# Head 0's later probability tile: normalised and turned by VectorE instead of GpSimd and TensorE

## The reference

```python
scores = jnp.einsum('bnhd,bmhd->bhnm', q, k) * scale
mask = jnp.tril(jnp.ones((n, n), bool))
scores = jnp.where(mask[None, None], scores, -jnp.inf)
p = jax.nn.softmax(scores, axis=-1)
o = jnp.einsum('bhnm,bmhd->bnhd', p, v).reshape(b, n, H * D)
```

## Time and profile before

| | |
|---|---|
| median of three runs | 1040.01 us |
| profiled execution, its own time | 1039.91 us |
| its span, first to last instruction | 1038.1 us |
| granted TensorE clock | 0.997 |
| first L1580 to the last of 128 | 27.1 to 825.7 us |
| eight steps, from L1580 to L1580 | 50.0 to 50.8 us |

### The profile page before, as it was taken

One profiled execution on the slowest core, in us unless ns is written; L12 is line 12 of the kernel. 1 busy time (PEld: TensorE's weight loads), 2 busy tenths in 40 slices (PEclk: granted clock), 3 DMA queues, 4 the chain that ended last, 5 costly groups with the idle time before them and its releaser, 6 DMA issues.

```text
span 1038.1 us, 25078 instructions
## 1 busy us (share of the span) xinstructions
PE 1021.4 (98%) x7827; PEld 981.6 (95%) x7827; DVE 827.1 (80%) x2841; ACT 868.2 (84%) x2399; POOL 931.4 (90%) x926
## 2 busy tenths in 40 slices
PE   7999999999999999999999999999999999999996
PEld 6899999999999999999999999999999999999996
DVE  6868888878887888788888888887777767677776
ACT  5988898989898989898989898889898867877774
POOL 4899999999999999999999999999999847877775
PEclk9999999999999999999999999999999999999998
DMA  7561121112112110121122112111131000000001
GB/s 262 187 184 43 42 63 41 43 52 68 44 36 61 63 42 33 62 63 42 33 68 67 42 39 75 43 42 53 42 113 31 2 1 11 22 24 29 22 22 41
DMA packets 35124, 58.56 MB, mean 56 GB/s; under 512 B 3136, under 2 KB 16000, under 8 KB 34688
## 3 DMA queue, kind: packets, MB, share of 16 engines
q1 hardware_dynamic: 34992, 56.96, 17.2%
HBM read 50.92 MB, written 9.18 MB: 58 GB/s over the span
## 4 chain that ended last, share of the span: by engine, by line
POOL 60%; PE 19%; issue 14%; DVE 1%; POOLq 0%; ACT 0%; ACTq 0%; DVEq 0%
POOL arena L599 15%; POOL arena L622 14%; POOL arena L633 13%; POOL arena L609 13%; PE psum L1017 12%; PE psum L1057 6%; POOL arena L581 1%; POOL arena L557 1%; POOL X L590 1%; PE psum L775 1%; PE psum L1030 1%; POOL arena L565 0%; PE psum L1039 0%; POOLq L303 0%; POOL arena L572 0%
## 5 line engine op out<-in xcount | busy, mean ns | idle before, releaser
L633 POOL TENSOR_TENSOR arena<-arena 128x768 f32<-128x768 f32 x128 | 196.2, 1533 | 8.9 <-DVE arena L1580 8.3
L609 POOL TENSOR_TENSOR arena<-arena 128x512 f32<-128x512 f32 x128 | 174.0, 1359 | 10.0
L1593 DVE SCALAR_TENSOR_TENSOR pt_split<-psum,vh_col,pt_split 128x256 fp32r<-128x256 f32 (+1 forms) x512 | 177.0, 407 | 3.5 <-ACT pt_split L1252 3.0
L599 POOL TENSOR_TENSOR arena<-arena,tables 128x512 f32<-128x512 f32 x128 | 166.9, 1304 | 13.7 <-ACT arena L1222 13.0
L622 POOL TENSOR_TENSOR arena<-arena 128x512 f32<-128x512 f32 x127 | 162.9, 1283 | 0.0
L929 PE MATMUL psum<-arena 128*128 128x256 f32 x512 | 153.9, 382 | 3.1 <-POOL arena L609 1.8
L775 PE MATMUL psum<-wo_hi,o_hi 128*128 128x256 f32 x512 | 152.1, 297 | 0.0
L1233 ACT ACTIVATE arena<-arena 128x256 f32<-128x256 f32 x256 | 128.6, 502 | 26.7 <-DVE arena L1570 20.1
L775 PE MATMUL psum<-xt_lo,wq_hi 128*128 128x256 f32 x512 | 144.7, 283 | 0.0
L775 PE MATMUL psum<-xt_hi,wq_lo 128*128 128x256 f32 x512 | 144.5, 282 | 0.0
L775 PE MATMUL psum<-wo_hi,o_lo 128*128 128x256 f32 x512 | 144.3, 282 | 0.0
(11 more groups left out here) (195 smaller groups left out, 3405.7 us busy)
## 6 DMA issues: line engine op xcount, KB each, us to landing
arena<-kh_rows SPq DMA_DIRECT2D x127, 256.0 KB, 3.3
out<-spare SPq DMA_DIRECT2D x15, 256.0 KB, 2.1
arena<-w_rows SPq DMA_DIRECT2D x6, 512.0 KB, 4.8
X<-L_attn_Wout SPq DMA_DIRECT2D x1, 2048.0 KB, 14.5
X<-L_attn_x SPq DMA_DIRECT2D x1, 2048.0 KB, 12.5
arena<-L_attn_Wq SPq DMA_DIRECT2D x1, 1536.0 KB, 10.0
X<-L_attn_x SPq DMA_DIRECT2D x1, 1536.0 KB, 9.7
w_rows<-L_ffn_w_gate_up SPq DMA_DIRECT2D x3, 512.0 KB, 8.2
```

What stands on the lines that cost most here:

```text
L599: nc.gpsimd.tensor_tensor(swap, swap, spread, ALU.mult).then_inc(q_sined, 1)
L609: nc.gpsimd.tensor_tensor(q_rot[p % 2], q_cos[p % 2], q_swap[p % 2], ALU.add).then_inc(q_roped, 1)
L633: nc.gpsimd.tensor_tensor(tb, tb, r.unsqueeze(3).to_broadcast([P, HP, 3, P]), ALU.mult).then_inc(p_ready, 1)
L1593: last = nc.vector.scalar_tensor_tensor(pt_lo[p % 2][:, o], b[:, i], vh[:, t, h:h + 1], pt_hi[p % 2][:, o].bitcast(F32), ALU.mult, ALU.sub ...
```

## The change

The later tile of the pair's first head (j = 0) leaves its old path. What is done now:

- The scores of head 0's later queries are written in another column order: the keys go through the PE in blocks of 32 columns ("b m c" order), and DVE's `maxima` uses a mask `mask_blocks` in that order.
- After the reciprocal, DVE multiplies this tile (128 x 256, in place in SBUF) by the reciprocal: `scale_late`, one TENSOR_SCALAR that waits for `p_inv`. It raises `p_scaled`.
- POOL's `normalise` covers the other 4 x 128 columns only and still waits for `p_inv`.
- SP issues four DMAs for each pair (`exchange`), SBUF to SBUF, 128 pieces of 256 bytes each, from `T` into the new tensor `blocks`, once `p_scaled` is there. They raise `p_exchanged`.
- In the next step, ahead of the next reciprocal, DVE turns `blocks` in 32 x 32 blocks into head 0's PSUM bank: `fill_pt`, one 128 x 256 transpose that waits for `p_exchanged` and for PE's one remaining transpose of head 0. It raises `pt_filled`.
- PE leaves out two of the six transposes of a pair; ACT's `split_pt` waits for `pt_filled` for head 0.

```diff
+            def exchange(g0, s):
+                at = pair_at(g0, s, LAG["softmax"])
+                if at:
+                    g, p, _ = at
+                    sp.wait_ge(p_scaled, g + 1)
+                    at_least(sp, pt_filled, g)
+                    for b in range(4):
+                        sp.dma_start(blocks[b * 32:(b + 1) * 32, :].rearrange("q (a e) -> q a e", a=4),
+                                     T[p % 2][:, 0, b * 64:(b + 1) * 64]).then_inc(p_exchanged, 16)
...
-                    tb = T[p % 2].rearrange("p j (c m) -> p j c m", m=P)
-                    r = rinv[p % 4].rearrange("p (j c) -> p j c", j=HP)[:, :, 0:3]
+                    tb = T[p % 2].rearrange("p j c -> p (j c)")[:, N:6 * P].rearrange("p (k m) -> p k m", m=P)
                     pool.wait_ge(p_inv, g + 1)
-                    nc.gpsimd.tensor_tensor(tb, tb, r.unsqueeze(3).to_broadcast([P, HP, 3, P]), ALU.mult).then_inc(p_ready, 1)
+                    nc.gpsimd.tensor_tensor(tb, tb, rinv[p % 4][:, 3:7].unsqueeze(2).to_broadcast([P, 4, P]), ALU.mult)\
+                        .then_inc(p_ready, 1)
...
-                        nc.tensor.matmul(sj[:, 0:2 * P], q[:, j, P:N], kt[:, j, :], start=True, stop=True,
+                        all_keys = kt[:, j, :] if j else kt[:, j, :].rearrange("p (m b c) -> p b m c", m=NT, b=4)
+                        nc.tensor.matmul(sj[:, 0:2 * P], q[:, j, P:N], all_keys, start=True, stop=True,
...
-                        nc.tensor.transpose(b[:, 0:P], tb[:, j, 2 * P:3 * P], ident[:, :])
-                        nc.tensor.transpose(b[:, P:2 * P], tb[:, j, 0:P], ident[:, :])
-                        nc.tensor.transpose(b[:, 2 * P:3 * P], tb[:, j, P:2 * P], ident[:, :]).then_inc(pt_ready, 1)
+                        last = nc.tensor.transpose(b[:, 0:P], tb[:, j, 2 * P:3 * P], ident[:, :])
+                        if j:
+                            nc.tensor.transpose(b[:, P:2 * P], tb[:, j, 0:P], ident[:, :])
+                            last = nc.tensor.transpose(b[:, 2 * P:3 * P], tb[:, j, P:2 * P], ident[:, :])
+                        last.then_inc(pt_ready, 1)
...
-                        act.wait_ge(pt_ready, head_count(g, j))
+                        act.wait_ge(*((pt_ready, head_count(g, j)) if j else (pt_filled, g + 1)))
...
                         at_least(dve, pt_ready, (g - 2) * HP + HP)
+                        at_least(dve, p_exchanged, (g - 2) * 64 + 64)
...
-                    nc.vector.tensor_tensor_reduce(tb[:, j, 0:2 * P], S_BANK[j][:, 0:2 * P], mask[:, :], -1.0, -MASKED,
+                    nc.vector.tensor_tensor_reduce(tb[:, j, 0:2 * P], S_BANK[j][:, 0:2 * P], (mask if j else mask_blocks)[:, :],
...
+            def scale_late(g0, s):
+                at = pair_at(g0, s, LAG["softmax"])
+                if at:
+                    g, p, _ = at
+                    late = T[p % 2][:, 0, 0:2 * P]
+                    dve.wait_ge(p_inv, g + 1)
+                    nc.vector.tensor_scalar(late, late, rinv[p % 4][:, 0:1], None, ALU.mult).then_inc(p_scaled, 1)
+
+            def fill_pt(g0, s):
+                at = pair_at(g0, s, LAG["turn"])
+                if at:
+                    g, p, _ = at
+                    dve.wait_ge(p_exchanged, g * 64 + 64)
+                    dve.wait_ge(pt_ready, head_count(g, 0))
+                    nc.vector.transpose(PT_BANK[0][:, P:3 * P].rearrange("p (m q a) -> p m a q", m=NT, a=4),
+                                        blocks[:, :].rearrange("p (a m c) -> p m a c", a=4, m=NT)).then_inc(pt_filled, 1)
...
+                    fill_pt(g0, s)
                     invert_sums(g0, s)
+                    scale_late(g0, s)
```

More of the change, by code:

```diff
@@ L109, in sandwich_kernel @@
         eps = sb("eps", [P, 1])
+        blocks = sb("blocks", [P, N])
+        mask_blocks = sb("mask_blocks", [P, N])
         cosq, sinq, cosk, sink = (tables[:, i, :] for i in range(4))
@@ L276, in sandwich_kernel @@
             sem(k) for k in ("s_ready", "s_max", "p_exp", "p_inv", "p_ready"))
+        p_scaled, p_exchanged, pt_filled = (sem(k) for k in ("p_scaled", "p_exchanged", "pt_filled"))
         pt_ready, pt_hi_done, pt_lo_done, o_ready, o_hi_done, o_lo_done, y_added = (
@@ L490, in batch @@
                         spread_kh(g0, s + KH_LEAD)
+                    exchange(g0, s)
                     if isinstance(g0, int) and g0 == 0 and s >= ROWS_STEP and s < ROWS_STEP + CHUNKS:
@@ L540, in _ @@
             nc.gpsimd.memset(minus_one, -1.0).then_inc(zeroed, 1)
-            pool.wait_ge(zeroed, 6)
+            nc.gpsimd.memset(mask_blocks[:, :], 0.0).then_inc(zeroed, 1)
+            pool.wait_ge(zeroed, 7)
             for m in (ident, ident_bf):
@@ L547, in _ @@
                                     pattern=[[-1, P]], channel_multiplier=1).then_inc(consts, 1)
+            late = mask_blocks[:, :].rearrange("p (b m c) -> p b m c", b=4, m=NT)[:, :, 1, :]
+            nc.gpsimd.affine_select(out=late, in_=late, compare_op=ALU.is_ge, fill=masked_fill, base=0,
+                                    pattern=[[-32, 4], [-1, 32]], channel_multiplier=1).then_inc(consts, 1)
             def invert_x(c0):
@@ L1134, in batch @@
                     early_unit_step(g0, s, step)
-            pe.wait_ge(consts, 3)
+            pe.wait_ge(consts, 2)
             keep_busy(F_BANK, 9)
@@ L1565, in maxima @@
                         at_least(dve, pt_ready, (g - 2) * HP + HP)
+                        at_least(dve, p_exchanged, (g - 2) * 64 + 64)
+                        if isinstance(g0, int) and g == 0:
+                            dve.wait_ge(consts, 4)
                     dve.wait_ge(s_ready, head_count(g, j))
                     nc.vector.memset(gate_mark[:, j:j + 1], 0.0)
-                    nc.vector.tensor_tensor_reduce(tb[:, j, 0:2 * P], S_BANK[j][:, 0:2 * P], mask[:, :], -1.0, -MASKED,
+                    nc.vector.tensor_tensor_reduce(tb[:, j, 0:2 * P], S_BANK[j][:, 0:2 * P], (mask if j else mask_blocks)[:, :],
+                                                   -1.0, -MASKED,
                                                    ALU.add, ALU.min, nmax[p % 4][:, 2 * j:2 * j + 1])
```

## The result

The changed kernel takes **1145.47 us** (median of 4 runs, 1145.14 to 1150.6), against 1040.07 us for the kernel before on the same chip. The ratio is 1.1023, with a 95% interval of 1.0999 to 1.1047: slower by 105.4 us. The forecast was 1155 us. The profiled execution has a span of 1143.6 us at a granted clock of 0.995, against 0.997 before, so TensorE's clock plays no part.

What follows compares the result with a forecast made beforehand. The prediction took a ring of waits between DVE and ACT, touched by PE at L1261, as the bound. 126 - 22 + 13 = 117 us on 1038.1, plus 1.8, gave 1157, stated as 1155; range 1040 to 1185.

Steps and rivals of the forecast that it cites:

- The exclusion: DVE's multiplication beside POOL's normalise: they exclude each other, so the multiplication ends 1.24 us after the reciprocal.
- One of the signs: In the profile after the change, PE would show gaps before L794; no size given.
- Who is first: At p_inv after the reciprocal: POOL starts after 0.08 us, DVE after 0.10, so POOL wins by 0.02; chance 0.45.
- DVE goes first: Rival at the reciprocal: DVE's multiplication starts before POOL's normalise, +55 us, 1095 us; chance 0.2.
- The sum: Whole kernel: 126 - 22 + 13 = 117 us added to a span of 1038.1 us.
- 159 - 33 - 22 = 104 us: DVE's multiplication: 128 x 1.24 = 159 us, less 33.2 idle before L1602, less 22 for 32 pairs with shorter waits.
- The turn: DVE's 32 x 32 transpose before the reciprocal: 0.42 us each, mostly in idle time, 13 us in all.
- PE's 28 us don't come off: PE's two dropped transposes per pair: 2 x 0.11 x 128 = 28 us of PE time, none of it gained.
- the ring: DVE and ACT waiting for each other set the pace, 5.63 us around in one step; PE touches it at L1261.
- The exchange is hidden: SP's four DMAs: exchanged at 4.5 us from the reciprocal's start, DVE needs it at 5.2; hidden by 0.6, costs nothing.
- No exclusion: Rival: DVE's multiplication runs at single rate through one port and doesn't exclude POOL; 1070 us, chance 0.17.
- Faster: Rival: PE is the bound and DVE's 211 us of idle time takes the new work; 1012 to 1020 us, chance 0.15.

Runs made afterwards that it cites:

- the experiment that makes it true: Changed kernel with DVE's multiplication also writing a row sum into a spare column, same operands, waits and place: 1065.21 us, ratio 1.0242.
- both-savings kernel: Kernel before with POOL's normalise on 512 columns and PE without two of six transposes, nothing in their place: 1018.11 us, ratio 0.9785.

## Why the prediction was right

**The exclusion was the main term, and its mechanism is shown** by four experiments: taking it away (two kernels) gives back 80.3 and 75.0 us, turning the order (two kernels) 74.3 and 77.1. The forecast had the multiplication end 1.24 us after the reciprocal. In the 95 pairs it ends 1.27 after it: normalisation from 0.079, 1.045 long, then 0.15. Uncontended it ends at 0.39 (forecast 0.35). One of the signs came out elsewhere: PE's gaps stand before its transposes (L966, 60.0 us), not before L794 (14.3 us).

The Trainium skill (SBUF — State Buffer, "Who interferes with whom") says that of the forms of tensor_scalar the one that also writes out its accumulator cannot enter the modes with both ports. The 479 ns beside POOL's 1043 agree with that rule, and the 1236 ns of the other form with its exclusive lock.

**Who is first: right by luck, from a wrong reading.** I let DVE's start come 0.10 us after the reciprocal, by the earlier trace rows, and POOL's 0.08, and gave POOL the port by 0.02 us. In the records L1616 starts 0.035 us after the reciprocal and POOL's L651 0.079, so DVE's record starts first by 0.044 us, and POOL still has the ports in 95 of 128 pairs. With POOL at 0.11 by its record, or at 0.16 by the memset's end, DVE has them. So the record's start doesn't say when DVE asks for the ports. If POOL's does, DVE asks later than 0.044 us after its own, and by 0.13 us at the latest; that is worked out from these three starts and not measured by itself. My margin of 0.02 us came out with the right sign, from a start (0.10 us) that L1616 doesn't show, and I had given this case no more than 0.45. *DVE goes first* was priced at 1095; the two kernels in which it is so measure 1071 and 1068. Of the 24 to 27 us too much, 12 are the remainders of L609, of which the mean of 508 ns leaves (508 - 353) x 128 = 20 us and not 32. The rest was not taken apart; slack that I didn't count, as in the sum below, is the likely part.

**The sum.** The multiplication stood in it with 159 - 33 - 22 = 104 us. Measured: mean end of the multiplication 1.112 us after the reciprocal, x 128 = 142 us, against 159 - 22 = 137 for the same thing in the forecast. The pairs with a shorter stay were 33 (32 in the forecast), shorter by 0.62 us on average (0.7 in the forecast). The idle time before `o_lo` (33.2) was used up as forecast: that wait is gone. That would leave 142 - 33 = 109 us. But the kernel that has this multiplication and neither exchange nor turn is 90.8 us above the kernel before (1130.9 against 1040.1). So the delay met more slack than the 33.2 us that I took off. DVE's rows show where, the kernel before first, then the kernel with the multiplication alone:

```profile
L1555 DVE TENSOR_TENSOR arena<-psum,tables 128x512 f32<-128x512 f32 x128 | 87.9, 687 | 7.8
...
L1602 DVE TENSOR_TENSOR o_lo<-psum,o_hi 128x512 fp32r<-128x512 f32 x128 | 87.4, 683 | 34.1 <-ACT o_hi L1261 33.2
```

```profile
L1575 DVE TENSOR_TENSOR arena<-psum,tables 128x512 f32<-128x512 f32 x128 | 86.5, 676 | 0.0
...
L1644 DVE TENSOR_TENSOR o_lo<-psum,o_hi 128x512 fp32r<-128x512 f32 x128 | 86.2, 673 | 1.8 <-ACT o_hi L1281 1.3
```

7.8 us of short waits before the cosine product are gone as well, and some 0.05 us in each of these two instructions, since their records overlap with the ones ahead where nothing is waited for: 14 us in all. 142 - 33 - 8 - 14 = 87 is near the 90.8.

The turn takes 0.45 us (0.42 in the forecast). Together with exchange and PE's saving it adds 14.6 us in the changed kernel (1130.9 to 1145.5), where I had 13 and nothing for the saving. 90.8 + 14.6 is the 105.4 measured. So of the 12 us by which 117 was too much, all and a little more lie in the multiplication's term, in slack that I left out. "PE's 28 us don't come off, since PE then waits for the ring" fits the changed kernel. It is wrong of the kernel before, where PE's and POOL's savings bring 22.0 us as a pair. What POOL's saving brings beside the multiplication no run shows; it is inside the 90.8.

**The exchange is hidden: right, with wrong parts.** Such a DMA takes SP 0.6 us to issue and not 0.40. SP's timeline:

```profile
332.72 2.48 SPq L490 DMA_DIRECT2D blocks<-arena  x4
335.25 0.59 SPq L479 DMA_DIRECT2D arena<-kh_rows  x1
```

It lands 1.9 us later (1.8 forecast), so that the last block is there 3.8 us after the multiplication, not 3.1. The turn waited for it only in 11 pairs, 14.2 us in all, 9.6 of them in the first eight pairs; I had nothing for it. Later the ring was 0.8 us longer in each pair (a batch of eight takes 55.3 and 58.4 us in turn, 50.0 to 50.8 before), which made the room.

**The other rivals.** *No exclusion*, at 1070: it doesn't apply to the form in the change, and the experiment that makes it true measures 1065.2. *Faster*, at 1012 to 1020: the both-savings kernel measures 1018.1, so the size was right for work that hides altogether, but even without exclusion the multiplication adds 37.5 us to that kernel with exchange and turn, 0.29 us in each pair, for an instruction that ends 0.51 us after the reciprocal. DVE's idle time, 211 us over the whole span, is not where the new work stands.

## What to carry to other kernels

Before moving work to VectorE beside GpSimd, ask which other instruction is released by the same semaphore: two that exclude each other and start on the same event met in 95 of 128 passes here, and the short one paid for the long one. If it must stand there, use a form that takes one port, though slower alone, or let the long one wait for the short one: a wait added to the engine with slack was worth 74 us here. And test savings together, and beside the work that takes their place: two that bring 2.7 and 4.5 us alone brought 22.0 as a pair, and PE's part of it didn't show once DVE multiplied.

## What was not expected of the hardware

- A race of less than a tenth of a microsecond decides 77 us: POOL's instruction at 0.079 us after the event shuts DVE out; behind a memset of 0.10 us it is shut out itself.
- VectorE's record of an instruction that waits for VectorE's own last one seems to start before it can touch SBUF: L1616 reads 353 ns and starts 0.035 us behind the reciprocal, where the forecast, from a pair with 0.10 us between them, had 0.10 and 0.25: nearly the same end (0.39 and 0.35).
- The one that stands still has part of its work behind it: DVE ends 0.15 us after POOL where it takes 0.35 alone, and POOL, with 0.28 us of its record beside DVE's multiplication, is lengthened by 0.14 (1.18 for 1.04).
- The form with the accumulator ran 479 ns in each of 128 pairs, beside POOL or not; the other form ranged from 353 to 1241.
- SP needed 0.6 us to issue each of the four DMAs of 32 KB, from SBUF to SBUF; the median landed in 1.9 us, the slowest in 7.0.
